# The output projection of the second attention in products of rounded high and low parts, summed over two turns instead of four

## The reference, cut to what matters

```python
NUM_HEADS, HEAD_DIM, LOCAL_HEADS = 32, 64, 30
q, k = apply_rope(q, k, pos, pos)
# heads 0 to 29: blocks of 128 queries, keys of the block and the 64 before it
# heads 30, 31: all keys up to the query
out = out.transpose(0, 2, 1, 3).reshape(B, L, NUM_HEADS * HEAD_DIM)   # 2048 wide
return jnp.einsum('blp,hp->blh', out, Wo) + bo                        # Wo: 256 x 2048
```

## Time and profile before

| what | value |
|---|---|
| time, three runs | 3140.01, 3140.96 (median), 3155.06 us |
| the profiled execution, its span | 3149.4 us |
| TensorE busy, share of the span | 3012.4 us, 96% |
| VectorE busy | 2118.6 us, 67% |
| ScalarE busy | 1863.2 us, 59% |
| GpSimd busy | 1017.1 us, 32% |
| the second attention | from about 1620 us to the end |
| products of `out`, line 1961 | 1024 records, 241.6 us |

### The profile page before, as it was taken

One profiled execution on the slowest core, in us unless ns is written; L12 is line 12 of the kernel. 1 busy time (PEld: TensorE's weight loads), 2 busy tenths in 40 slices (PEclk: granted clock), 3 DMA queues, 4 the chain that ended last, 5 costly groups with the idle time before them and its releaser, 6 DMA issues. The chain is left out here.

```text
span 3149.4 us, 66407 instructions
## 1 busy us (share of the span) xinstructions
PE 3012.4 (96%) x23638; PEld 2264.0 (72%) x23638; DVE 2118.6 (67%) x5888; ACT 1863.2 (59%) x4638; POOL 1017.1 (32%) x1627
## 2 busy tenths in 40 slices
PE   7999999999999999997988999999999999999998
PEld 5888888853444444434877888788887888788886
DVE  5666666678989989975655555655556555555556
ACT  4666666647877778773445555455554555455553
POOL 0000000001100000001016666576656666566663
PEclk9999999989999999998999999999999999999999
DMA  4111111232333232103224444344443444244432
GB/s 150 50 48 48 48 48 41 60 68 44 69 50 64 35 75 45 30 9 116 83 69 110 99 101 94 103 122 101 94 107 93 114 103 95 67 114 105 102 87 68
DMA packets 296707, 246.35 MB, mean 78 GB/s; under 512 B 149180, under 2 KB 231740, under 8 KB 296252
## 3 DMA queue, kind: packets, MB, share of 16 engines
q1 hardware_dynamic: 296380, 242.11, 31.7%
HBM read 100.71 MB, written 44.04 MB: 46 GB/s over the span
## 5 line engine op out<-in xcount | busy, mean ns | idle before, releaser
L1838 ACT ACTIVATE b_pp<-b_pp,b_nm 128x192 f32<-128x192 f32 (+2 forms) x1024 | 472.8, 463 | 447.6 <-DVE b_nm L2005 366.1
L1007 ACT ACTIVATE a_pt<-ps 128x512 f32<-128x512 f32 x1024 | 556.1, 595 | 178.9 <-PE ps L1043 177.9
L176 DVE TENSOR_REDUCE mx<-ps 128x2 f32<-128x1024 f32 x512 | 622.3, 1224 | 58.6 <-PE ps L167 44.0
L1808 POOL TENSOR_SCALAR b_pp<-b_pp,b_rc 128x192 f32<-128x192 f32 x960 | 389.2, 428 | 383.9 <-DVE b_rc L2014 383.9
L2026 DVE COPY b_pt<-ps 128x384 f32<-128x384 f32 (+2 forms) x336 | 182.1, 556 | 316.7 <-PE ps L1927 301.4
L2005 DVE CUSTOM_DVE_ANT_0 b_pp<-ps,b_mk 128x192 f32<-128x192 f32 x960 | 276.3, 354 | 136.8 <-PE ps L1906 136.8
L797 DVE SCALAR_TENSOR_TENSOR f_yac<-ps,f_cw,f_yac 128x128 f32<-128x128 f32 x992 | 278.1, 344 | 125.3 <-PE ps L596 123.0
L596 PEld LDWEIGHTS ps<-w,f_sq 128*128 128x128 f32 x2048 | 265.2, 191 | 26.5 <-issue 6.0
L596 PE MATMUL ps<-w,f_sq 128*128 128x128 f32 x2048 | 270.2, 275 | 0.3
L1961 PE MATMUL ps<-b_wo,b_oT 128*128 128x256 f32 x1024 | 241.6, 380 | 3.7 <-ACT b_vv L1831 3.7
L1056 PE MATMUL ps<-a_pt,a_v 128*32 128x256 f32 x3072 | 242.0, 395 | 0.0
(11 more groups left out here) (282 smaller groups left out, 7332.8 us busy)
## 6 DMA issues: line engine op xcount, KB each, us to landing
b_rt<-b_qf SPq DMA_DIRECT2D x1024, 64.0 KB, 2.0
qk_parts<-f_aa SPq DMA_DIRECT2D x32, 512.0 KB, 2.7
v_rows<-f_va_ SPq DMA_DIRECT2D x16, 512.0 KB, 2.8
rl<-in_W1qT SPq DMA_DIRECT2D x64, 128.0 KB, 2.6
rl<-in_W1kT SPq DMA_DIRECT2D x64, 128.0 KB, 2.7
rl<-in_W1vT SPq DMA_DIRECT2D x32, 256.0 KB, 3.2
b_wo<-in_W1oT SPq DMA_DIRECT2D x16, 512.0 KB, 4.2
b_vs<-b_vv SPq DMA_DIRECT2D x60, 128.0 KB, 2.9
```

The costliest lines, as they stand in the source:

```text
L176: e.tensor_reduce(M["mx"][kh % 3][:, :, jt, h], P.pair(s), AX.X, ALU.max, negate=True).then_inc(P.free_sem(s), 1)
L1007: e.activation(pt[(4 * i + 2 * j + a) % 12][:, :], P.ap((*s, a)), ACT.Exp).then_inc(P.free_sem((*s, a)), 1)
L1808: m = e.tensor_scalar(x, x, r[:, 2 * u + h:2 * u + h + 1], 1.0, ALU.mult, ALU.mult)
L1838: e.activation(x, x, ACT.Exp, bias=nm[n % 4][:, c:c + 1], scale=-1.0, accum_out=sm[n % 4][:, c:c + 1]).then_inc(exp_done, 1)
```

## The change

- `out` is due after every second turn and sums two turns; there are 256 of them instead of 128. Each is two `mm3`, six products of rounded parts instead of four fp32 products.
- Two `out` stand at the end of a local stride, one at the end of every second stride of a full turn. *store* takes both tiles of the stride before.
- The attention output is kept as a high part `oh` (ScalarE, the old *evac*) and a low part `ol` (*evac_low*, VectorE, at the end of the stride's list), four turns deep. Bank 7 is now given free by *evac_low*.
- The weights come two turns at a time into one buffer, and are split by *wo_high* (ScalarE) and *wo_low* (GpSimd) in the last two slots of odd turns.
- The descriptor scratch of the program is set to 8192 bytes.

```diff
+        if n >= 0 and n % 2:
+            out[6].append(("wo_high", n // 2))
+            out[7].append(("wo_low", n // 2))
...
         out += evacs
+        out += [("evac_low", x[1]) for x in out if x[0] == "evac"]
         return out
...
+        if n % 2 == 0:
+            p.append(("load_wo", n // 2))
...
-            if store:
-                p.append(store.pop())
-            if side and (not last or j % 2):
-                p.append(side.pop(0))
-                if p[-1][1] % 4 == 3:
-                    store.append(("store", *p[-1][1:]))
-        if at % 4 == 3:
-            p.append(("wo", n // 4))
-            side += [("out", n // 4, t) for t in range(NQ)]
+            p += store
+            store = []
+            for _ in range(j % 2 if last else 2):
+                if side:
+                    p.append(side.pop(0))
+                    if p[-1][1] % GB == GB - 1:
+                        store.append(("store", *p[-1][1:]))
+        if at % 2:
+            side += [("out", n // 2, t) for t in range(NQ)]
...
-                        if t >= 8:
-                            w.wait_ge(*P.filled(("out", t // 4 - 2, 4 * half + 3)))
-                        e.activation(oT[:, t % 8, half * CH:(half + 1) * CH], P.ap(o),
-                                     ACT.Copy).then_inc(P.free_sem(o), 1)
+                        if t >= 4:
+                            w.wait_ge(*P.filled(("out", t // 2 - 2, 4 * half + 3)))
+                        e.activation(oh[:, t % 4, half * CH:(half + 1) * CH], P.ap(o), ACT.Copy).then_inc(oh_ready, 1)
...
-                    w.wait_ge(wo_in[n % 2], 16 * (n // 2 + 1))
-                    w.wait_ge(*P.emptied(("o", 4 * n + 3, t // 4)))
-                    for c in range(4):
-                        m = e.matmul(P.ap(s)[:, 0:256], oT[:, n % 2 * 4 + c, t * 128:(t + 1) * 128], wo[n % 2][:, c, :],
-                                     start=c == 0, stop=c == 3)
+                    w.wait_ge(wo_low, n + 1)
+                    w.wait_ge(*P.emptied(("o", 2 * n + 1, t // 4)))
+                    for c in range(2):
+                        x, tok = (2 * n + c) % 4, slice(t * 128, (t + 1) * 128)
+                        m = mm3(e, P.ap(s)[:, 0:256], oh[:, x, tok], ol[:, x, tok], woh[n % 2][:, c, :],
+                                wol[n % 2][:, c, :], c == 0, c == 1)
...
+                elif k == "evac_low":
+                    t, i = strides[n]
+                    if not whole(t) or i % 4 == 3:
+                        o, x, tok = ("o", t, i // 4), t % 4, slice(i // 4 * CH, (i // 4 + 1) * CH)
+                        w.wait_ge(oh_ready, 2 * t + i // 4 + 1)
+                        e.tensor_tensor(ol[:, x, tok], P.ap(o), oh[:, x, tok].bitcast(F32),
+                                        ALU.subtract).then_inc(P.free_sem(o), 1)
```

More of the change, by code:

```diff
@@ L25 @@
 NTURN = B * NP
-ACT_TURNS = (0, 1, 2, 3)
+GB = NP // 2
 class Waits:
@@ L1540, in second_attention_plan @@
         for f in fourths(at):
-            p += [f, ("evac", f[1])]
+            p += [f, ("evac", f[1]), ("evac_low", f[1])]
         if at < s:
@@ L1633, in second_attention @@
         pt = [sb(f"pt{i}", [128, 4, 128]) for i in range(5)]
-        oT = sb("oT", [128, NP // 2, L])
-        wo = [sb(f"wo{i}", [128, 4, 256]) for i in range(2)]
+        oh, ol = sb("oh", [128, 4, L], FR), sb("ol", [128, 4, L], FR)
+        wor = sb("wor", [128, 2, 256])
+        woh = [sb(f"woh{i}", [128, 2, 256], FR) for i in range(2)]
+        wol = [sb(f"wol{i}", [128, 2, 256], FR) for i in range(2)]
         acc = sb("acc", [128, NQ, 256])
@@ L1646, in second_attention @@
         vb_in = [sem(f"vb_in{i}") for i in range(2)]
-        wo_in = [sem(f"wo_in{i}") for i in range(2)]
+        wo_in, wo_high, wo_low, oh_ready = sem("wo_in"), sem("wo_high"), sem("wo_low"), sem("oh")
         gx_in = [sem(f"gx_in{i}") for i in range(2)]
@@ L1736, in sync @@
                                     qf[x % 2][32 * j:32 * j + 32, :]).then_inc(rt_in[x % 3], 16)
[L1737 to L1741, removed]
+                elif k == "load_wo":
+                    w.wait_ge(wo_low, n)
+                    e.dma_start(wor[:, :, :], wo_t[:, n % GB * 2:n % GB * 2 + 2, :]).then_inc(wo_in, 16)
+                    if n % GB == GB - 1:
                         for t in range(2):
-                            fetch(e, w, n // 4, t)
+                            fetch(e, w, n // GB, t)
                 elif k == "store":
-                    b, t = n // 4, s[2]
+                    b, t = n // GB, s[2]
                     r = slice(b * L + t * 128, b * L + (t + 1) * 128)
@@ L1761, in gated @@
         def gated(e, w, s):
-            b, t = s[1] // 4, s[2]
+            b, t = s[1] // GB, s[2]
             u = 8 * b + t
@@ L1793, in pool @@
                     e.tensor_tensor(y[:, t], y[:, t], rt[x % 3][:, :], ALU.add).then_inc(added[s[2]], 1)
-                elif k == "out" and n % 4 == 3 and n // 4 < B - 1:
+                elif k == "wo_low":
+                    w.wait_ge(wo_high, n + 1)
+                    e.tensor_tensor(wol[n % 2][:, :, :], wor[:, :, :], woh[n % 2][:, :, :].bitcast(F32),
+                                    ALU.subtract).then_inc(wo_low, 1)
+                elif k == "out" and n % GB == GB - 1 and n // GB < B - 1:
                     gated(e, w, s)
@@ L1824, in scalar @@
                     e.activation(vh[n % 2][:, :, :], vraw[:, :, :], ACT.Copy).then_inc(v_high, 1)
+                elif k == "wo_high":
+                    w.wait_ge(wo_in, 16 * (n + 1))
+                    if n >= 2:
+                        w.wait_ge(*P.filled(("out", n - 2, NQ - 1)))
+                    e.activation(woh[n % 2][:, :, :], wor[:, :, :], ACT.Copy).then_inc(wo_high, 1)
                 elif k == "values":
@@ L2027, in vector @@
                                           P.ap(f)[:, lo:hi]).then_inc(P.free_sem(f), 1)
+                elif k == "evac_low":
[5 more added lines that the diff above has]
+                                        ALU.subtract).then_inc(P.free_sem(o), 1)
                 elif k == "out":
-                    b, g, t = n // 4, n % 4, s[2]
+                    b, g, t = n // GB, n % GB, s[2]
                     p = P.ap(s)[:, 0:256]
@@ L2037, in vector @@
                     e.tensor_tensor(acc[:, t, :], p, acc[:, t, :], ALU.add).then_inc(P.free_sem(s), 1)
-                    if n == 4 * B - 1:
+                    if n == GB * B - 1:
                         gated(e, w, s)
@@ L2175 @@
     from concourse.bass_utils import run_bass_kernel_spmd
-    nc = bacc.Bacc("TRN2", target_bir_lowering=False, num_devices=1)
+    nc = bacc.Bacc("TRN2", target_bir_lowering=False, num_devices=1, dynamic_dma_scratch_size=8192)
     arrays, A = {}, {}
```

## The result

| | before | changed |
|---|---|---|
| time, median | 3141.99 us (3140.01 to 3155.06) | 3224.02 us (3211.92 to 3232.48) |
| ratio | | 1.0249, interval 1.0226 to 1.0272 |
| profiled execution, its span | 3149.4 us | 3222.7 us |
| TensorE busy | 3012.4 us, 96% | 3000.4 us, 93% |
| mean granted clock over the span | 0.987 | 0.979 |

The change costs 2.5%. That is slower, as forecast, but above the range of 3145 to 3213. I again took the stride lengths, the distances between the starts of two *first* steps, and summed them by kind for both profiled executions. "Forecast" is what the terms of the prediction make for the same strides.

The account below looks back on a forecast made before the run. TensorE, 96% busy, was taken to bound the kernel. Terms -43.9 + 1.6 + 48.2 + 40 + 2.4 = +48 us on the median 3140.96 gave 3189 us, with an 8-in-10 range of 3145 to 3213.

Parts of the forecast that it names:

- Both waits: Second attention: 28 output steps wait for bank 7's low part, +48.2 us; nine gated strides wait for gate rows, 36.9 us.
- wo_high*, *wo_low* and the tail: Weight splitting falls where ScalarE and GpSimd idle over 3 us, costing nothing; the tail saves at most 1, taken as 0.
- the full turns: Four full-attention turns: quicker steps save 0.6, VectorE gets 0.6 to 1.2 more; +0.6 us each, +2.4 together.
- Two gated output steps a stride: Last group of a batch: gate-row fetches come late and stall TensorE, 4.1 us nine times, plus GpSimd's late work; together +40.
- GpSimd's late work behind it: Second of three gated strides: GpSimd's rope sum ready after the next scores want it, 0.9 us a batch, 2.7.
- a rival at 0.12: TensorE's clock falls in each of nine gated stalls, costing some 3.4 us each, 31 more: 3220 us; chance 0.12.
- The saving on TensorE: Output steps at the end of 107 local strides: 2.15 us becomes 1.74, 0.41 saved each, -43.9 us.
- the clock's case: TensorE's clock falls in the nine gated stalls: 3220 us, chance 0.12.
- the last rival: Products of rounded parts don't issue at 0.12 us, so two output steps take 2.15 as before: 3233 us; chance 0.04.

Follow-up runs that it names:

- The first edit: Stores and the fetches after them issued ahead of the next stride's slots instead of behind them, against the changed kernel: 3167.21 us.
- the second: Output steps of a group begun one stride later, against the changed kernel: 3190.01 us; together with stores and fetches moved ahead of the stride, 3117.36 us.
- the fp32 experiment: Each output step as two fp32 products of the high parts, against the kernel with both edits (stores and fetches earlier, output steps later): 3150.22 us.

## Why the prediction was wrong

**Both waits were the right ones.** They have the places, numbers and causes that were forecast: 28 waits for the low part at 12.28 - 10.55 = 1.73 each (forecast 1.72), nine stalls on the gate's fetches with transposes at S'+9.4 on the mean (9.0). The first edit gives back 57 us, and the second gives back 50 on top of it. *wo_high*, *wo_low* and the tail cost nothing that shows, and the full turns +2.1 for +2.4.

**The step that failed most is "Two gated output steps a stride", 40 us.** It measured 58. The stall itself, forecast at 36.9, came out at 40.4, and GpSimd's late work behind it, forecast at 2.7, at 4.8. The remaining 13.2 are what failed: the sum went on at full clock, and the case in which it doesn't stood as a rival at 0.12.

I had two facts for that: the clock is low at the end of a wait of 7.2 us, and stays at 1.00 through gaps of 1 to 2 us. For 4 us "no row decides", I wrote, and weighed it as unlikely. That was a poor reading of the trace of before. The rows put the wait from 1669.68 to 1676.87 and the fall at 1672.90, so the clock fell 3.2 us into the wait, not after 7.2. And there was a wait of 4 us to look at, where this attention begins. In the timeline, and by windows:

```profile
1626.41 0.76 PE L107 MATMUL ps<-xh,w1b_h 128*128 128x512 f32 x1 [4.26 <-PEq L1407]
```

```profile
1625.14:1631.96 6.82, 5.54 (x19) 5.00 (x20) 2.56 (x6) 0.00 (x0) 2.78 (x4) 0.50 0.37 98
```

TensorE waited from 1622.15 to 1626.41, and the clock fell at 1625.14, 3.0 us into that wait. A wait of 3.92 us in the first stage (32.23 to 36.15) has the same, with the fall at 34.53. These were the rows that I said were missing, and they spoke for the fall. So did the Trainium skill's rule on bursts that begin after a wait for a transfer ("TensorE: Matmul & The Clock Gate", HAM oscillation); the trace after agrees in nine of nine, with stalls of 4.3 us on the mean. The rival's time, 3220, is near 3224 partly by luck: it took 31 us for the clock where 13.2 were lost.

**The saving on TensorE was mis-sized**: "0.41 us, 10.85 becomes 10.44" measured 0.30. The step counted 0.12 per product up to the next scores. The interval ahead of the scores is 0.09 longer, and it was already inside the 2.15 that I subtracted from, which runs to the start of the scores. Counted alike, both have the same entry and exit, and what is left is twelve products of 0.12, 1.43 us, for four of 0.43, 1.73. The timeline of before has

```profile
2307.37 1.46 PE L1961 MATMUL ps<-b_wo,b_oT 128*128 128x256 f32 x6
```

and its fourth record at 2308.02, so 0.217 a record and two records a product. The difference is 0.30, as the fp32 experiment measured. Over 107 strides it is 0.11 x 107 = 12 us; 7.3 of it are in the row of the 69 strides. (The sum with 0.12 a product makes 1.77 and not the 1.76 that I wrote; the forecast used 1.74, so nothing hangs on it.)

**The base.** I put +48 on the median, 3141. Spans differ by 73.3, medians by 82.0. The remaining 8.7 is of the size of the 8.4 by which the profiled span of before lies above its median. No pair of profiles can place it: the start of the second attention, behind stages that all these kernels share, moves by up to 8.7 us against before in the profiles of the experiments.

So of the 35 us between 3189 and 3224, 18 are in the gated strides (13 of them the clock), 7 in the missing 0.11 with small terms of both signs, 8.7 between executions, and 1 in the base, whose median came out at 3141.99. The range ended at 3213, below the clock's case and the last rival, which held 0.16 together. Without the 13.2 of the clock the time would have been 3211, just inside it.

## What to carry to other kernels

Where several transfers and a dependent chain share one in-order queue, look at where the *last* fetch stands relative to its use when the work per step doubles: moving the stores and fetches ahead of the stride was worth 57 us here. When a buffer is given free by a different engine than before, find the first instruction that reads it fresh, and put one stride between them. And when a forecast contains stalls of the engine that bounds the kernel, search the whole trace of before for a wait of that length, other stages included, and see what the clock does in it. Here it fell in the two waits of 3.9 and 4.3 us of the kernel before, and with nine of nine of 3.8 to 4.9 us after the change.

## What the runs showed of the hardware that was not expected

- Products of rounded parts, 128x256 moving, issue every 0.12 us; an fp32 product of the same size takes 0.43. Three of the one do the work of one of the other in 0.36, so 17% is won, where the two steps as a whole (entry and exit included) win 14% of 2.15.
- Scores with 64 rows stationary start 0.09 us later than the pace behind rounded products and 0.17 later behind transposes. The order around them moves this cost, but doesn't remove it.
- The low clock came also with shorter waits: in seven of nine with waits of 2.15 to 3.49 us (2.6 on the mean), and in eight of nine with 2.5 to 3.5. A wait of 2.15 had it and one of 2.85 didn't.
- 44 us at 1.2 GHz cost 13 us, not the half of 44, as TensorE waited in part of them.
